# Inversion on 64-row diagonal blocks, 32-column matmul tiles, roots split between two engines, and a new order of the steps

## The chip, the core and the metric

The kernel runs on one core of one Trainium2 chip. A core has TensorE (PE in the profile; its weight loads are shown as PEld), VectorE (DVE), ScalarE (ACT), GpSimd (POOL) and SyncE (SP), which issues the DMAs. The metric is the device time of one launch in microseconds.

## What is computed

Two blocks run on x of 2048 tokens by 128 features, and each adds its layer-normalised result to x. The first is an online linear regression that is scanned over the tokens; the second is a stack of six layers, each with attention in windows of 32 tokens (16 heads of 64) and a gated feed-forward of 341 hidden units.

```python
def step(W, inp):
    xt, vt = inp
    y = xt @ W.T
    err = y - vt
    gW = scale * (err.T @ xt)
    return (W - eta * gW, y)
...
# attention, per layer
q = l2norm(q) * qs
k = l2norm(k) * ksc
q = q * cos * scale + rotate_half(q) * sin * scale
k = k * cos * inv + rotate_half(k) * sin * inv
out = local_attention(q, k, v)
...
# feed-forward, per layer
xn = (x - mu) / jnp.sqrt(var + 1e-05) * g + bln
a, gate = jnp.split(xn @ W1 + b1, 2, -1)
return a * jax.nn.gelu(gate, approximate=False) @ W2 + b2
...
for i in range(DEPTH):
    x = attn_layer(shift_tokens(x), ...) + x
    x = ffn_layer(shift_tokens(x), ...) + x
```

## The kernel before

The 2048 tokens are 16 tiles of 128 tokens; four tiles are a group.

**Prologue.** The scan is done in chunks of 128 tokens. Each chunk needs the inverse of a lower triangular 128x128 matrix, unit diagonal plus a scaled Gram matrix. `gram` makes the Gram matrices, VectorE turns them into starting matrices `c_mm`, and six rounds (`ROUNDS`) double the size of the inverted blocks from 2 to 128. In round r GpSimd multiplies the scaled Gram matrices by a level mask (`c_b`), TensorE multiplies them with the inverse so far (`below`, L355), ScalarE copies the product out of PSUM (`c_q`), TensorE multiplies from both sides (`update`, L371 and L372), and VectorE subtracts (L699). Four groups of four matrices go through each round. Then `apply_x` and `apply_v` use the inverses, and sixteen short `chain_w`, `chain_d` products carry W from chunk to chunk, the last twelve of them inside the first steps of the main loop.

**Main loop.** All five engines run a loop over s. For tile t of 96 (`STEPS`, six layers of 16 tiles) TensorE does in turn: `project` for k and for q (L245, x with a 128x1024 half of the weights, into `psq`), `turn` (L253, sixteen 64x64 transposes of q or of k), `mask` (L276, starts `pss` with the mask), `scores` (L284), `turn_p` (L253, transposes of the probabilities), `values` (L265, four banks, one per window of 32 tokens, which already hold v times the output weights), and `mix` (L300, probabilities times those). Once per group come `F` and `X` (four 128x128 transposes each, L521 and L530), `hidden` for three blocks of the gate (G0 to G2) and of the value (A0 to A2) of the feed-forward (L310), `narrow` (Z, L317) and, for the coming layer, one `merge` (H, L326), which multiplies a quarter of v's weights with the output weights.

The order within one s, and by how many steps each piece lags, is written out by hand for every engine. `take` hands out four PSUM banks (`ring`) in TensorE's order, so a use waits until the use four places earlier has been read out (`freed`). `psq` is one pair of banks for both projections: q of a tile waits until ScalarE has squared k (`sq_k`), and k of the next tile until it has squared q (`sq_q`).

VectorE multiplies both projections by the rotation tables (L782, L785, L841, L857), reduces squares, row maxima and sums. GpSimd adds the two rotary products (L1236, L1245), multiplies q and k by the inverse norms (L1290, L1294) and the probabilities by their inverse sums (L1240), makes the table `tab`, and computes the inverse norms `rn`: from a seed that ScalarE makes of the exponent bits, ten small instructions on 128x32 (L1269 to L1287). ScalarE copies PSUM banks to SBUF and does Square, Exp and Gelu. All data are f32 except the mask, which is bf16. One f32 matmul is two records in the trace (two passes), a transpose is one.

## Time and profile before

| | us |
|---|---|
| median of 3 runs | 1675.6 |
| lowest, highest | 1674.8, 1677.26 |
| profiled execution, whole time | 1674.12 |
| profiled execution, its span | 1672.3 |
| PE busy in the span | 1591.6 (95%) |
| POOL busy | 1386.3 (83%) |
| DVE busy | 1253.5 (75%) |
| ACT busy | 1080.7 (65%) |
| PE busy from 300 to 1500 us | 1194.84 of 1200 |

The span is what the trace covers, from the first to the last instruction; the whole time holds 1.8 us more. The share of busy time is an average over the prologue (up to the first `project` at 113.59 us), the main loop and a tail. A PE row of the timeline reads: start, length from the start of the first to the end of the last of its instructions, line, what is written and read, the part of the array used (rows*columns), the shape moved, and how many records. Its end lies some 0.16 us behind the moment at which the next instruction can enter, so costs are read from start to start.

### The profile page before, as it was taken

The numbers are of one execution on the slowest core, as the hardware profiler recorded it, in microseconds if no ns is written. First come the engines' busy times: TensorE is split into PE (matmuls) and PEld (weight loads), VectorE is DVE, ScalarE is ACT, GpSimd is POOL, SyncE is SP. The second block draws the span as 40 slices with busy tenths as digits, with TensorE's granted clock in tenths as the row PEclk, the third lists the DMA queues.
The fourth block names the chain that finished last, engine by engine and source line by source line (L and its number), as shares of the span: only waits on it lengthen the run. The fifth ranks groups of instructions, "written<-read, shape, count | busy, mean of one in ns | idle before, by whom it ended". The sixth has DMA issues, their size and how long they took to land.

```text
span 1672.3 us, 67208 instructions
## 1 busy us (share of the span) xinstructions
PE 1591.6 (95%) x29072; PEld 938.3 (56%) x29072; DVE 1253.5 (75%) x1683; ACT 1080.7 (65%) x1843; POOL 1386.3 (83%) x1726
## 2 busy tenths in 40 slices
PE   5986899999999999999999999999999999999994
PEld 4963455655555555565555555555555555555552
DVE  5447777777787787787787787777777787778863
ACT  3234766767766776766766767676766766766661
POOL 6318898988988988988998988988998998988971
PEclk9987999999999999999999999999999999999998
DMA  5000000010000010000010000010000000000000
GB/s 191 2 26 1 28 9 8 3 59 9 3 22 9 3 59 9 3 21 9 3 59 9 3 22 9 3 59 9 3 22 9 2 10 9 4 21 9 7 11 26
DMA packets 24534, 32.70 MB, mean 20 GB/s; under 512 B 2372, under 2 KB 21424, under 8 KB 23344
## 3 DMA queue, kind: packets, MB, share of 16 engines
q1 hardware_dynamic: 24240, 28.41, 5.2%
q8 instruction: 230, 3.77, 0.9%
q14 instruction: 64, 0.52, 0.1%
HBM read 21.06 MB, written 1.05 MB: 13 GB/s over the span
## 4 chain that ended last, share of the span: by engine, by line
PE 82%; POOL 8%; issue 5%; DVE 3%; ACT 1%; DMA 0%; SPq 0%; POOLq 0%; DVEq 0%; ACTq 0%
PE psq L245 19%; PE ring L265 18%; PE ring L253 9%; PE ring L300 9%; PE ring L310 8%; PE pss L284 7%; PE ring L317 3%; PE pss L276 1%; PE ring L326 1%; PE ring L355 1%; POOL qa L1290 1%; POOL qa L1245 1%; POOL qa L1236 1%; POOL qa L1294 1%; POOL pr L1240 1%
## 5 line engine op out<-in xcount | busy, mean ns | idle before, releaser
L245 PE MATMUL psq<-wqk,x0S 128*128 128x512 f32 x768 | 383.0, 622 | 5.5 <-ACT x0S L990 3.7
L265 PE MATMUL ring<-mh,x0S 128*32 128x512 f32 x3072 | 367.2, 595 | 0.4 <-ACT uT L1158 0.4
L1245 POOL TENSOR_TENSOR qa<-qa,qb 128x1024 f32<-128x1024 f32 x96 | 228.3, 2378 | 65.6 <-DVE qb L857 65.5
L1236 POOL TENSOR_TENSOR qa<-qa,qb 128x1024 f32<-128x1024 f32 x96 | 226.9, 2364 | 6.8 <-DVE qb L785 6.8
L245 PEld LDWEIGHTS psq<-wqk,x0S 128*128 128x128 f32 x768 | 136.1, 192 | 133.0 <-issue 117.2
L253 PEld LDWEIGHTS ring<-ident,qa 64*128 64x128 f32 x3072 | 110.5, 139 | 158.8 <-issue 104.7
L866 DVE TENSOR_REDUCE ss<-sq 128x16 f32<-128x1024 f32 x96 | 117.1, 1220 | 104.0 <-ACT sq L1062 104.0
L300 PE MATMUL ring<-u,pT 128*32 128x128 f32 x6144 | 187.6, 274 | 3.8 <-ACT pT L1129 3.5
L1290 POOL TENSOR_TENSOR qa<-qa,rn 128x1024 f32<-128x1024 f32 x96 | 182.7, 1903 | 7.5
L1240 POOL TENSOR_TENSOR pr<-pr,rden 128x1024 f32<-128x1024 f32 x96 | 184.0, 1916 | 2.0 <-DVE rden L814 2.0
L1294 POOL TENSOR_TENSOR qa<-qa,rn 128x1024 f32<-128x1024 f32 x96 | 183.2, 1908 | 0.0
L300 PEld LDWEIGHTS ring<-u,pT 128*32 128x32 f32 x6144 | 162.0, 110 | 27.2 <-issue 27.2
L284 PEld LDWEIGHTS pss<-kT,qT 64*32 64x32 f32 x12288 | 127.9, 105 | 83.3 <-issue 82.2
L782 DVE TENSOR_TENSOR qa<-psq,tab 128x1024 f32<-128x1024 f32 x96 | 117.2, 1221 | 75.4 <-PE psq L245 75.2
L1051 ACT COPY qT<-ring 128x512 f32<-128x512 f32 x96 | 56.3, 586 | 157.3 <-PE ring L253 157.3
L265 PEld LDWEIGHTS ring<-mh,x0S 128*32 128x32 f32 x3072 | 87.9, 109 | 123.1 <-issue 107.4
L841 DVE TENSOR_TENSOR qa<-psq,tab 128x1024 f32<-128x1024 f32 x96 | 117.2, 1221 | 51.1 <-PE psq L245 51.1
L310 PE MATMUL ring<-xh,w 128*128 128x512 f32 (+1 forms) x288 | 146.7, 620 | 1.4 <-ACT xh L1147 0.9
L284 PE MATMUL pss<-kT,qT 64*32 64x64 f32 x12288 | 144.5, 226 | 3.3 <-issue 3.3
L253 PE MATMUL ring<-ident,qa 64*128 64x64 f32 x3072 | 136.7, 229 | 6.4 <-POOL qa L1290 5.3
L1062 ACT ACTIVATE sq<-psq 128x1024 f32<-128x1024 f32 x96 | 98.3, 1023 | 67.7 <-DVE qb L857 67.7
L1167 ACT ACTIVATE sq<-psq 128x1024 f32<-128x1024 f32 x96 | 97.8, 1018 | 65.6 <-DVE qb L785 65.6
(161 smaller groups left out, 3005.1 us busy)
## 6 DMA issues: line engine op xcount, KB each, us to landing
wqk<-in_wqk SPq DMA_DIRECT2D x6, 1024.0 KB, 4.8
mvT<-in_mvT SPq DMA_DIRECT2D x6, 512.0 KB, 3.6
wo<-in_wo SPq DMA_DIRECT2D x6, 512.0 KB, 5.0
xf<-x SPq DMA_DIRECT2D x24, 128.0 KB
xf<-x SPq DMA_DIRECT2D x24, 127.0 KB
rope<-in_rope SPq DMA_DIRECT2D x1, 2048.0 KB, 10.2
w<-in_w SPq DMA_DIRECT2D x6, 341.0 KB, 7.1
xmid<-in_x SPq DMA_DIRECT2D x4, 256.0 KB, 5.4
```

The source lines that it names most:

```text
L245: return mm(psq[:, 512 * (n % 2):512 * (n % 2) + 512], x0S[:, tile * P:tile * P + P], wqk[:, l % 2, 512 * n:512 * n + 512], start=True, st ...
L253: last = tr(banks[r][:, 64 * blk:64 * blk + 64], src(blk)[rows], ident[rows, rows])
L265: last = mm(bank[WIN * g:WIN * g + WIN, :], x0S[:, tile * P + WIN * w:tile * P + WIN * w + WIN], mh[:, l % 2, g, :, :].rearrange("p j n -> ...
L284: last = mm(pss[WIN * w:WIN * w + WIN, 512 * r + KEYS * pair:512 * r + KEYS * pair + KEYS], qT[rows, pair, WIN * w:WIN * w + WIN], kT[rows ...
L300: last = mm(bank[WIN * w:WIN * w + WIN, 0:P], pT[:, half, b * P + WIN * w:b * P + WIN * w + WIN], u4[:, slot, v_w, b * P:b * P + P], start ...
L310: return mm(bank[0:n, :], w1[:, col:col + n], xnT[:, :], start=True, stop=True)
L782: v.tensor_tensor(a3[t % 2][:, 16:32, :], q3, tab[:, t % 2, 2, :].unsqueeze(1).broadcast_to([P, HEADS, HD]), ALU.mult)
L1236: g_.tensor_tensor(qa[:, t % 2, 1024:2048], qa[:, t % 2, 1024:2048], qb[:, 1024:2048], ALU.add).then_inc(sum_k, 1)
L1240: g_.tensor_tensor(p4[t % 2], p4[t % 2], rden[:, :].unsqueeze(1).unsqueeze(3).broadcast_to([P, 2, HEADS, WIN]), ALU.mult).then_inc(p_ready, 1)
L1245: g_.tensor_tensor(qa[:, t % 2, 0:1024], qa[:, t % 2, 0:1024], qb[:, 0:1024], ALU.add).then_inc(sum_q, 1)
L1290: g_.tensor_tensor(a3[t % 2][:, 16:32, :], a3[t % 2][:, 16:32, :], rn[:, 16:32].unsqueeze(2).broadcast_to([P, HEADS, HD]), ALU.mult).then_ ...
L1294: g_.tensor_tensor(a3[t % 2][:, 0:16, :], a3[t % 2][:, 0:16, :], rn[:, 0:16].unsqueeze(2).broadcast_to([P, HEADS, HD]), ALU.mult).then_inc ...
```

## The change

1. **Inversion on blocks of 64.** Rounds 0 to 4 work on the two 64x64 diagonal blocks of each matrix alone, at the two diagonal quarters of the array; the starting matrices, masks, copies and subtractions are 64 columns wide instead of 128. The last round makes only the off-diagonal block from the two inverted ones and writes it into `c_inv`, whose rest GpSimd has set to zero in round 1.
2. **Start.** TensorE's first transposes wait for the identity alone, VectorE's coefficient for eta and the level masks, and is asked for after the second group's statistics instead of the first's. The level masks are half as large.
3. **32-column tiles.** `project`, `hidden` and `narrow` issue each matmul as four (for the last 85 hidden units three) with 32 output rows each, as `values` and `mix` did before.
4. **Mask.** Eight 64-row, 32-column matmuls in the tiles that `scores` uses, issued directly before `scores`; before, two 32-row, 128-column ones were issued before `mix`, and two 128x128 ones in a layer's first tile.
5. **Merges** come in pairs that use the two 64-row halves of the array in turn, every second group.
6. **Roots.** Another polynomial: seven small instructions on ScalarE (the seed among them, which was there before) and three on GpSimd, instead of one and ten.
7. **New order.** Every engine's loop is written out anew and is five steps longer (`STEPS + 19` for `STEPS + 14`; the first projection is at s = 2). `project` for k stands near the end of a step, for q near the middle of the next. The three Gelus of a group stand at three places of ScalarE's loop instead of together. G0 to A2 are spread over the steps, Z moves to a step with X and F, and the final normalisation of the last layer's groups lies five steps behind its statistics.

```diff
             def project(t, n):
 
                 tile, l = t % TILES, t // TILES
-                return mm(psq[:, 512 * (n % 2):512 * (n % 2) + 512], x0S[:, tile * P:tile * P + P],
-                          wqk[:, l % 2, 512 * n:512 * n + 512], start=True, stop=True)
+                for w in range(NWIN):
+                    last = mm(psq[WIN * w:WIN * w + WIN, 512 * (n % 2):512 * (n % 2) + 512],
+                              x0S[:, tile * P + WIN * w:tile * P + WIN * w + WIN],
+                              wqk[:, l % 2, 512 * n:512 * n + 512], start=True, stop=True)
+                return last
 
...
             def mask(t):
 
-                for h in range(2):
-                    if t % TILES == 0:
-                        mm(pss[:, 512 * h:512 * h + 512], ident16[:, :], mask16[:, 1, :], start=True, stop=False)
-                    else:
-                        rows = slice(WIN * h, WIN * h + WIN)
-                        mm(pss[:, 512 * h:512 * h + 512], rep16[rows, :], mask16[rows, 0, :], start=True, stop=False)
+                for w in range(NWIN):
+                    for r in range(2):
+                        rows = slice(HD * r, HD * r + HD)
+                        mm(pss[WIN * w:WIN * w + WIN, 512 * r:512 * r + 512], rep16[rows, WIN * w:WIN * w + WIN],
+                           mask16[rows, int(t % TILES == 0 and w == 0), :], start=True, stop=False)
 
...
-                return mm(bank[0:n, :], w1[:, col:col + n], xnT[:, :], start=True, stop=True)
+                for c in range(0, n, WIN):
+                    m = min(WIN, n - c)
+                    last = mm(bank[c:c + m, :], w1[:, col + c:col + c + m], xnT[:, :], start=True, stop=True)
+                return last
 
...
                 for k in range(QUAD):
                     for j, (h0, n) in enumerate(HBLK):
                         n += j == 2
-                        last = mm(bank[:, k * P:k * P + P], uT[0:n, j, k * P:k * P + P], w2[0:n, j, :],
-                                  start=(j == 0), stop=(j == 2))
+                        for w in range(NWIN):
+                            rows = slice(WIN * w, WIN * w + WIN)
+                            last = mm(bank[rows, k * P:k * P + P], uT[0:n, j, k * P + WIN * w:k * P + WIN * w + WIN],
+                                      w2[0:n, j, :], start=(j == 0), stop=(j == 2))
                 return last
...
-            def merge(bank, j):
-
-                rows = slice(HD * (j % 2), HD * (j % 2) + HD)
+            def merge(what, l):
+
+                banks = [take("H%d" % j, l) for j in what]
+                for bank, n in banks:
+                    wait(pe, freed[bank], n)
                 for k in range(4):
-                    pair = 4 * (j // 2) + k
-                    last = mm(bank[:, k * P:k * P + P], mvT[rows, pair, :], wo[rows, pair, :], start=True, stop=True)
-                return last
+                    for j, (bank, n) in zip(what, banks):
+                        rows = slice(HD * (j % 2), HD * (j % 2) + HD)
+                        pair = 4 * (j // 2) + k
+                        last = mm(ring[bank][:, k * P:k * P + P], mvT[rows, pair, :], wo[rows, pair, :], start=True, stop=True)
+                        if k == 3:
+                            last.then_inc(filled[bank], 1)
...
-                    last = mm(quarter[g][:, k, :], c_xT[:, g, k, :], c_xT[:, g, k, :], start=True, stop=True)
+                    for o in range(2):
+                        for p in range(2):
+                            last = mm(blocks[g][BOTH[p], o, k, :], c_xT[:, g, k, BOTH[p]], c_xT[:, g, k, BOTH[p ^ o]],
+                                      start=True, stop=True)
...
-                    last = mm(rbank[g][:, k, :], c_b[r % 2][:, g, k, :], c_mm[:, g, 1, k, :], start=True, stop=True)
+                    if r < ROUNDS - 1:
+                        for rows in BOTH:
+                            last = mm(rblock[g][rows, k, :], c_b[r % 2][rows, g, k, :], c_mm[rows, g, 1, k, :], start=True, stop=True)
+                    else:
+                        last = mm(rblock[g][LO, k, :], c_g[HI, g, 1, k, :], c_inv[HI, g, k, HI], start=True, stop=True)
                 last.then_inc(a_Q, 1)
...
                     if r < ROUNDS - 1:
-                        mm(bank[:, k * P:k * P + P], c_q[:, g, k, :], c_mm[:, g, 0, k, :], start=True, stop=True)
-                    last = mm(bank[:, 512 + k * P:512 + k * P + P], c_mm[:, g, 0, k, :], c_q[:, g, k, :],
-                              start=True, stop=True)
+                        for rows in BOTH:
+                            mm(blocks[g][rows, 0, k, :], c_q[rows, g, k, :], c_mm[rows, g, 0, k, :], start=True, stop=True)
+                        for rows in BOTH:
+                            last = mm(blocks[g][rows, 1, k, :], c_mm[rows, g, 0, k, :], c_q[rows, g, k, :], start=True, stop=True)
+                    else:
+                        last = mm(blocks[g][LO, 1, k, :], c_mm[LO, g, 0, k, :], c_q[LO, g, k, :], start=True, stop=True)
                 last.then_inc(a_U, 1)
...
-                    lo = 512 * (r == ROUNDS - 1)
-                    both = c_mm[:, g].rearrange("p t k n -> p (t k n)")[:, lo:]
-                    v.tensor_tensor(both, both, pair[g % 2][:, lo:], ALU.subtract).then_inc(a_m, 1)
+                    if r < ROUNDS - 2:
+                        v.tensor_tensor(c_mm[:, g], c_mm[:, g], blocks[g], ALU.subtract).then_inc(a_m, 1)
+                    elif r == ROUNDS - 2:
+                        wait(dve, s_iz, 1)
+                        v.tensor_tensor(c_mm[:, g, 0], c_mm[:, g, 0], blocks[g][:, 0], ALU.subtract)
+                        for rows in BOTH:
+                            last = v.tensor_tensor(c_inv[rows, g, :, rows], c_mm[rows, g, 1], blocks[g][rows, 1], ALU.subtract)
+                        last.then_inc(a_m, 1)
+                    else:
+                        v.tensor_scalar(c_inv[LO, g, :, HI], blocks[g][LO, 1], -1.0, None, ALU.mult).then_inc(a_m, 1)
...
-                if g == 0:
-                    dve.wait_ge(s_const, 16 * NCONST)
+                if g == 1:
+                    dve.wait_ge(s_level, 32)
...
+                    nc.scalar.activation(rg[:, :].bitcast(I32), ssc[:, :].bitcast(I32), ACT.Copy, bias=SEED,
+                                         scale=-0.5).then_inc(seed_ready, 1)
+                    act.wait_ge(seed_ready, t + 1)
+                    wait(act, rb_ready, t)
+                    nc.scalar.activation(ra[:, :], rg[:, :], ACT.Square).then_inc(rg_ready, 1)
...
+                    act.wait_ge(rb_ready, t + 1)
+                    nc.scalar.activation(rs1[:, :], rb[:, :], ACT.Square, bias=rcon[:, 0:1]).then_inc(rs_ready, 1)
+                    nc.scalar.activation(rs2[:, :], rb[:, :], ACT.Square, bias=rcon[:, 1:2]).then_inc(rs_ready, 1)
+                    wait(act, rp_ready, t)
+                    act.wait_ge(rs_ready, 2 * t + 1)
+                    nc.scalar.activation(rf1[:, :], rs1[:, :], ACT.Copy, bias=RB)
+                    act.wait_ge(rs_ready, 2 * t + 2)
+                    nc.scalar.activation(rf2[:, :], rs2[:, :], ACT.Copy, bias=R4 * RD, scale=R4).then_inc(rf_ready, 1)
...
+                    pool.wait_ge(rg_ready, t + 1)
+                    wait(pool, rs_ready, 2 * t)
+                    g_.tensor_tensor(rb[:, :], ra[:, :], ssc[:, :], ALU.mult).then_inc(rb_ready, 1)
...
+                    pool.wait_ge(rf_ready, t + 1)
+                    g_.tensor_tensor(rp[:, :], rf1[:, :], rf2[:, :], ALU.mult).then_inc(rp_ready, 1)
+                    pool.wait_ge(rp_ready, t + 1)
+                    g_.tensor_tensor(rn[:, :], rg[:, :], rp[:, :], ALU.mult).then_inc(rn_ready, 1)
...
-                    g_.tensor_tensor(ra[:, :], rn[:, :], rn[:, :], ALU.mult).then_inc(r_step, 1)
...
-                    g_.tensor_tensor(rn[:, :], rc[:, :], ra[:, :], ALU.mult).then_inc(r_step, 1)
```

TensorE, one step of the main loop. The first name is the tensor written, then what it reads; 32x512 is output rows by columns. Before, starting at the mask of one tile:

```order
L276 MATMUL pss<-mask,rep 128x512 x2
L300 MATMUL ring<-u,pT 32x128 x32
L265 MATMUL ring<-mh,x0S 32x512 x4
L253 MATMUL ring<-ident,qa 128x64 x16
L245 MATMUL psq<-wqk,x0S 128x512 x2
L253 MATMUL ring<-ident,qa 128x64 x16
L265 MATMUL ring<-mh,x0S 32x512 x12
L284 MATMUL pss<-kT,qT 32x64 x64
L253 MATMUL ring<-ident,pr 128x64 x16
```

and now, starting at a hidden block (L323 is `hidden`, L311 `mix`, L265 the transposes, L255 `project`, L277 `values`, L286 the mask, L295 `scores`):

```order
L323 MATMUL ring<-xh,w 32x512 x4
L311 MATMUL ring<-u,pT 32x128 x32
L265 MATMUL ring<-ident,qa 128x64 x16
L255 MATMUL psq<-wqk,x0S 32x512 x8
L265 MATMUL ring<-ident,qa 128x64 x16
L277 MATMUL ring<-mh,x0S 32x512 x4
L323 MATMUL ring<-xh,w 32x512 x4
L277 MATMUL ring<-mh,x0S 32x512 x4
L286 MATMUL pss<-mask,rep 32x512 x8
L295 MATMUL pss<-kT,qT 32x64 x64
L265 MATMUL ring<-ident,pr 128x64 x16
L255 MATMUL psq<-wqk,x0S 32x512 x8
```

The 128-wide projections and hidden blocks have gone, and the mask has moved from in front of `mix` to in front of `scores`.

ScalarE, a step with Gelus. Before, all three stand behind one table load (`pr` is Exp, `uT` Gelu, `sq` the square that frees `psq`):

```order
L1110 COPY pT<-ring 128x8x64
L1129 COPY pT<-ring 128x8x64
L1134 ACTIVATE pr<-pr 128x1024
L1158 ACT_TABLE_LOAD
L1158 ACTIVATE uT<-ring,par 128x512 x2
L1158 ACTIVATE uT<-ring,par 85x512
L1167 ACTIVATE sq<-psq 128x1024
L1174 ACTIVATE kT<-kT,kfac 128x8x32
```

and now, the end of one such step and the start of the next:

```order
L1223 COPY u<-ring 128x512
L1228 ACTIVATE sq<-psq 128x1024
L1085 ACT_TABLE_LOAD
L1085 ACTIVATE uT<-ring,par 85x512
L1093 COPY kT<-ring 128x8x64
L1099 COPY kT<-ring 128x8x64
```

The third Gelu has a table load of its own between the square and the copies of k; the whole program has 92 table loads where it had 46.

## Rows read from the trace of the kernel before

**Rows 1.** The page: span, and the chain that ended last, by engine.

```profile
span 1672.3 us, 67208 instructions
PE 82%; POOL 8%; issue 5%; DVE 3%; ACT 1%; DMA 0%; SPq 0%; POOLq 0%; DVEq 0%; ACTq 0%
```

**Rows 2.** Busy time by stretch: us, PE, PEld, DVE, ACT, POOL, PEclk, DMA, GB/s.

```profile
44.00:90.00 46.00, 46.00 (x414) 46.00 (x413) 21.50 (x19) 11.04 (x20) 14.89 (x12) 1.00 0.01 1
300.00:1500.00 1200.00, 1194.84 (x22912) 679.35 (x22914) 940.76 (x1161) 837.50 (x1414) 1068.00 (x1314) 1.00 0.05 16
```

**Rows 3.** Timeline of TensorE over one step: start, length, line, tensors, array part.

```profile
1012.86 1.04 PE L265 MATMUL ring<-mh,x0S 128*32 128x512 f32 x8
1013.84 0.71 PE L253 MATMUL ring<-ident,qa 64*128 64x64 f32 x16
1014.48 1.98 PE L245 MATMUL psq<-wqk,x0S 128*128 128x512 f32 x4
1016.30 1.02 PE L310 MATMUL ring<-xh,w 128*128 128x512 f32 x2
1017.25 0.71 PE L253 MATMUL ring<-ident,qa 64*128 64x64 f32 x16
1017.89 2.78 PE L265 MATMUL ring<-mh,x0S 128*32 128x512 f32 x24
1020.60 1.49 PE L284 MATMUL pss<-kT,qT 64*32 64x64 f32 x128
1022.02 1.12 PE L310 MATMUL ring<-xh,w 128*128 128x512 f32 x2
1023.08 0.71 PE L253 MATMUL ring<-ident,pr 64*128 64x64 f32 x16
1023.72 1.98 PE L245 MATMUL psq<-wqk,x0S 128*128 128x512 f32 x4
1025.63 0.39 PE L276 MATMUL pss<-mask,rep 32*128 32x512 bf16 x2
1025.95 1.96 PE L300 MATMUL ring<-u,pT 128*32 128x128 f32 x64
1027.72 1.04 PE L265 MATMUL ring<-mh,x0S 128*32 128x512 f32 x8
```

**Rows 4.** Timeline of TensorE: the product Z of a group.

```profile
1040.55 2.84 PE L317 MATMUL ring<-w,uT 128*128 128x128 f32 x24
```

**Rows 5.** Groups of instructions by line: all merges (busy us, mean ns).

```profile
L326 PE MATMUL ring<-wo,mvT 64*128 64x128 f32 x192 | 27.9, 285 | 0.6 <-issue 0.6
```

**Rows 6.** Timeline of ScalarE: copy of the probabilities, table load, Exp, square.

```profile
1024.30 0.59 ACT L1129 COPY pT<-ring 128x512 f32<-128x512 f32 x1
1024.91 1.28 ACT L1134 ACT_TABLE_LOAD   x1
1026.21 1.06 ACT L1134 ACTIVATE pr<-pr 128x1024 f32<-128x1024 f32 x1
...
1028.13 1.02 ACT L1167 ACTIVATE sq<-psq 128x1024 f32<-128x1024 f32 x1 [0.86 <-DVE qb L785]
```

**Rows 7.** Timeline of GpSimd: first of ten small root instructions, and what follows them.

```profile
1022.61 0.24 POOL L1269 TENSOR_TENSOR ra<-rn 128x32 f32<-128x32 f32 x1
...
1025.82 1.90 POOL L1290 TENSOR_TENSOR qa<-qa,rn 128x1024 f32<-128x1024 f32 x1
```

**Rows 8.** Timeline of VectorE: the second rotary product of k.

```profile
1026.88 1.22 DVE L785 TENSOR_TENSOR qb<-psq,tab 128x1024 f32<-128x1024 f32 x1
```

**Rows 9.** The chain that ended last, in the prologue: start us, us, what.

```profile
5.51 6.38 DMA mh<-in_bv
...
45.85 3.57 PE ring L355 x32
...
88.73 3.57 PE ring L355 x32
...
113.59 2.08 PE psq L245 x2
```

More of the change, by code:

```diff
@@ L387, in apply_x @@
                 for k in range(QUAD):
[L388 removed]
+                    last = mm(rbank[bank][:, k, :], c_xn[:, g, k, :], c_inv[:, g, k, :], start=True, stop=True)
                 last.then_inc(filled[bank], 1)
@@ L427, in features @@
                 last.then_inc(filled[bank], 1)
-            def first_merge(j):
-                bank, n = take("H%d" % j, 0)
-                pe.wait_ge(mw_ready, 32)
-                wait(pe, freed[bank], n)
-                merge(ring[bank], j).then_inc(filled[bank], 1)
+            pe.wait_ge(s_ident, 16)
             turn_in(0)
@@ L625, in _ @@
-                if i >= 0:
-                    bank, n = take("A1", i)
-                    wait(pe, freed[bank], n)
-                    hidden(ring[bank], 1, 0).then_inc(filled[bank], 1)
-                t = s - 2
-                if 0 <= t < STEPS:
-                    banks = [take("P0", t), take("P1", t)]
-                    pe.wait_ge(p_ready, t + 1)
-                    for bank, n in banks:
-                        wait(pe, freed[bank], n)
-                    turn_p([ring[bank] for bank, n in banks], t)
@@ L1186, in _ @@
+                    rows = HBLK[0][1]
+                    nc.scalar.activation(uT[0:rows, 0, :], ring[bank][0:rows, :], ACT.Gelu,
+                                         bias=par[0:rows, i // GROUPS, 5:6]).then_inc(freed[bank], 1)
         @block.gpsimd
```

948 lines of the change are left out of this document (489 added, 459 removed).

## The prediction

> **What bounds the kernel now.** I read the shares of the chain first: TensorE carries 82% of it, "issue" 5%, GpSimd 8% [rows 1]. Then the busy time by stretch: from 300 to 1500 us TensorE is busy 1194.84 of 1200 us, while GpSimd has 1068, VectorE 941 and ScalarE 838 [rows 2]. So in the loop nothing but TensorE's own stream sets the pace, and a change is worth what it takes out of that stream, as long as no new wait appears. Third, the timeline of one step, read from start to start [rows 3]. From the values at 1012.86 to the next at 1027.72 are 14.86 us; two hidden blocks in it took 0.95 (1016.30 to 1017.25) and 1.06 (1022.02 to 1023.08), which leaves 12.85 for a step without extras. Last, the chain in the prologue, which takes 113.59 us before the first projection [rows 9].
>
> **32-column tiles for projections and hidden blocks.** The row of four full-width passes is 1.98 long, that of two 1.12: one more pass costs 0.43. The row of 24 tile records (six rounds of four) is 2.78, that of eight (two rounds) 1.04: one more round costs 0.435 [rows 3]. So the arithmetic is no faster in tiles. By the Trainium skill, "TensorEngine Tiling (Array Packing)", section Theoretical Speedup, packing gains where a dimension is 64 or less; by that rule this edit, whose dimensions are 128, brings nothing, and for the passes the trace agrees. What is left to gain are the changes between array shapes. Beyond its passes, the projection in front of the mask takes 1.91 - 1.72 = 0.19, that in front of a turn or hidden block 0.10; values in front of a turn 0.98 - 0.86 = 0.12, in front of the scores 2.71 - 2.58 = 0.13; a hidden block that comes after scores and before a turn 1.06 - 0.86 = 0.20, one that comes after a projection 0.09 [rows 3]. So leaving a shape costs about 0.12, and entering the full array about 0.1 more. A turn (0.64) and the scores (1.41) can't be divided that way; I give them the same 0.13. A step has nine changes of shape before (mask to mix, values to turn, turn to q, q to turn, turn to values, values to scores, scores to turn, turn to k, k to mask) and seven after, since mix, values, projections and hidden blocks now share one shape and mask and scores another. Lower bound: two changes at 0.13, 0.26. Upper bound: also 0.1 for each of the two projections that no longer enter the full array, 0.46. I take 0.35, because rows 3 show the entry cost for hidden blocks but for projections only mixed with the neighbour's. The mask's own time (0.32 to the mix, of which 0.21 is half of an f32 pass) stays; eight tiles side by side stream it once. Four steps of a group: **1.4 us**.
>
> **Other edits of the group.** A merge costs 27.9 / 24 = 1.16 [rows 5]; two of them on the two row halves run like the turn's pairs, so a pair costs about one: between 0.3 and 0.58 saved per group, I take 0.4. Z's 24 records take 2.84 [rows 4], about 0.112 each; as tiles they run like the mix, 64 records or 16 rounds in 1.77, 0.111 each [rows 3]: 24 rounds 2.66, 0.1 saved. Against that, X now stands between mix and turn and F between turn and projection, each a visit to the full array at about 0.2, where they stood behind a full-width projection at no cost; the hidden block behind the scores, at 0.2, is gone: minus 0.2. Sum 1.4 + 0.4 + 0.1 - 0.2 = **1.7 us per group**. All of it lies on the path. The stream sets the end for about 23 of the 24 groups (filling and emptying the pipeline are set by latencies, and I take the new depth of lags there as neutral, plus or minus 6): 39 us.
>
> **Roots.** Ten small GpSimd instructions take 1025.82 - 1022.61 = 3.21 us per step [rows 7], three will take 1.0. GpSimd is off the path, so its 2.2 us bring nothing themselves; the cover is TensorE's stream. Six more small ones on ScalarE, some 0.25 each, raise its 838 of 1200 us (10.8 per step) to 12.3. The chain from turned probabilities to the next turn of k is copy 0.59, seed, square, GpSimd's product, four on ScalarE, two on GpSimd, scaling 1.90: about 5.2 us with their hand-overs (0.08 between two rows of GpSimd). TensorE has between the two the k projection, U3, U0, a hidden block and the mix, 1.86 + 0.86 + 0.86 + 0.86 + 1.77 = 6.2. It fits by 1.0.
>
> **New order, and what is queued on ScalarE.** Gelus at three places double the table loads, from 46 to 92, two more per group. A load takes 1.30 from its start to that of the Exp behind it [rows 6]. Take E as the end of TensorE's U3. ScalarE copies U3 from E+0.2 to E+0.8, loads the table to E+2.1, does Exp (1.06) to E+3.15, copies U0 to E+3.6 and squares k (1.02; neighbours overlap by 0.1) to E+4.55. `psq` then is free for q. TensorE wants it after U0, a hidden block, the mix and the turn: 0.86 + 0.86 + 1.77 + 0.64 + 0.12 = E+4.25. It waits 0.3, in the two steps of a group whose Exp comes behind a Gelu. In one of these a third load and Gelu stand between the square and the copies, to about E+6.55; the bank they free is wanted by the turn of q at E+6.4: 0.15 more. Sum 0.7 per group, 16 us. In the other two steps the square is ready 1.0 early. Bounds: 0 (the table could load during another wait) and 1.4 (the same shortfalls doubled, since each of them is a small difference of long sums). VectorE's rotary products stay at 1.22 each [rows 8]; two of them and the square of q (1.02) fit between the projection of q and that of k with 2 us to spare.
>
> **Prologue.** (a) The first transposes wait for the last constant, which lands at 5.51 + 6.38 = 11.9 [rows 9]; now for the identity and for the first group's normalised rows: 0 to 6 us, I take 5. (b) The weight rows L355 from 45.85 to 88.73 are four rounds, 10.72 us each [rows 9], in which TensorE is busy 46 of 46 us at a granted clock of 1.00, its 2.4 GHz level [rows 2]: 96 records of 128 columns, 0.112 each. After, 192 records of 64 columns, in pairs on two diagonal quarters. The nearest row is the turn, eight pairs of 64 columns in 0.64 less 0.13, 0.064 a pair [rows 3]: 96 pairs are 6.1, at best (half of a 128-column record) 5.4. Saved 4.6 to 5.3, I take 4.9: 20 for four rounds. VectorE and GpSimd, 21.5 and 14.9 of 46 us there, halve too and stay covered. (c) Round 0 and the start of round 1, from 11.9 to 45.85, are short TensorE pieces between VectorE's and GpSimd's products; these become half as wide: 34 us less the 5 of (a) that just shifts; between 8 and 18 less, I take 13. (d) The last round: 3.57 for `below` and as much for `update`, each about halved or better, 4. Together **42 us**, on the path entirely, bounds 28 and 50.
>
> **Sum.** Against the profiled execution: span 1672.3, 1.8 us around it. 42 + 39 - 16 = 65 us less: span 1607, time 1609; the profiled execution lies 1.5 under the median of 1675.6, so the median becomes **1610 us**.
>
> **Rivals.** (1) No new wait on ScalarE: the loads fall into its idle time. For it: ScalarE is idle 30% of the loop [rows 2]. Against: the load stands in order between U3's copy and the Exp. 1610 - 16 = 1594. (2) The diagonal quarters don't run side by side, or the thinner work leaves the engine at its 1.2 GHz level: a round stays near 11. For it: no row of before has 64x64 parts. Against: transposes on two row halves and values on four column parts do run side by side. 1610 + 20 = 1630. (3) The shape changes are not what costs, and the step keeps its 12.85: 1.4 x 23 = 32 more, 1642. Against: 0.09 and 0.20 for the same hidden block in two places [rows 3]. (4) Slower: the root chain, now with six hand-overs between ScalarE and GpSimd and as many within them, becomes the loop's clock. It fits by 1.0 only; it decides once it is 1.0 + 65/96 = 1.7 us longer than laid out, that is if a hand-over costs 0.25 instead of 0.08 over some ten of them. At 0.27 each it would be 1.9 longer, 0.9 per step, 86 less the 65: about 1697. Against: ScalarE rows follow GpSimd's and VectorE's within 0.1. (5) Slower too: a change of table costs more than the load's row. If the engine also stood still around it for as long again, q would wait 1.6 twice a group and the turn 1.5: 4.8 a group, 110 - 81 = 29 above before, 1705. The row speaks against it: 1.28 long, 0.02 behind the copy, 0.02 ahead of the Exp [rows 6]. The Trainium skill, "ScalarE: Activation LUTs", section What ACT_TABLE_LOAD costs, gives about 2.66 us for a switch, a drain included; by that rule this rival holds, and this trace shows 1.30.
>
> **How the numbers follow.** Forecast (1598 to 1624) 0.46; rival 1 0.26; rival 2 0.12; rival 3 0.08; rival 4 0.04; rival 5 0.02; another slower one or no change 0.02. The range goes from rival 1 with the prologue at its better bound (1594 - 8, rounded to 1585) to rival 3, 1643. About 0.2% of the time, 3.4 us, is what a measurement of this kernel can tell from no change. Faster 0.93, same 0.01, slower 0.06.
>
> **What would show each step.** The first projection at 70 to 73 us instead of 113.6; weight loads of `below` some 5.8 apart per round; a step without extras near 12.5, and four steps about 1.0 shorter; a projection of two banks 1.72 to 1.75 between neighbours of its own shape; TensorE idle, or a lengthened first pass of q, behind ScalarE's square only in steps with a table load; 92 table loads; GpSimd's busy time down by about 160 us and ScalarE's up by about 200. The prediction is wrong if rounds stay at 10 us, if idle time of TensorE in the loop exceeds 1.5 us per group, or if the steps take 12.85 as before.

## The result and the profile after

| | before | after |
|---|---|---|
| median | 1676.4 us (4 runs) | 1627.4 us (4 runs) |
| lowest, highest | 1674.8, 1678.9 | 1622.7, 1628.3 |
| ratio after/before, 95% interval | | 0.9701 [0.9678, 0.9723] |
| span of the profiled execution | 1672.3 us | 1620.9 us |

49 us faster; 65 were forecast. The first page lines of the changed kernel, answering [rows 1] (span, busy time by engine, chain by engine):

```profile
span 1620.9 us, 79276 instructions
PE 1532.9 (95%) x35024; PEld 853.4 (53%) x35024; DVE 1243.1 (77%) x1693; ACT 1219.7 (75%) x2368; POOL 1220.0 (75%) x1051
PE 75%; issue 9%; ACT 7%; DVE 1%; POOL 1%; DMA 0%; SPq 0%; ACTq 0%; DVEq 0%; POOLq 0%
```

TensorE's share of the chain fell from 82% to 75%, and ScalarE, which had 1%, now has 7%. The same in the busy times by stretch, answering [rows 2] (us, PE, PEld, DVE, ACT, POOL, PEclk, DMA, GB/s): inversion rounds, then the loop.

```profile
34.00:54.00 20.00, 20.00 (x692) 20.00 (x689) 9.92 (x17) 6.36 (x16) 4.81 (x7) 1.00 0.02 5
300.00:1500.00 1200.00, 1174.11 (x27354) 641.65 (x27346) 946.63 (x1174) 956.87 (x1844) 951.82 (x780) 1.00 0.05 16
```

TensorE now stands idle 25.9 of 1200 us in the loop; before it was 5.2. That is 1.07 more per group of tiles.

**Where the 49 us come from.** The start of the k projection of a tile, before minus after: tile 0 35.3 us (113.59 to 78.28), tile 4 38.5, tile 8 44.2, tile 16 47.1, tile 48 45.6, tile 92 49.0, end 51.4. So the prologue brought 35, the filling of the pipeline 12, and the long loop almost nothing: its mean period per group (tiles 16 to 92, 19 groups) is 61.84 us before and 61.75 after. (These are the profiled executions; that of the changed kernel is the fastest of its four, so the differences end at 51.4 and not at 49.)

One step of TensorE after the change, answering [rows 3]:

```profile
898.86 1.92 PE L255 MATMUL psq<-wqk,x0S 128*32 128x512 f32 x16
900.60 1.90 PE L277 MATMUL ring<-mh,x0S 128*32 128x512 f32 x16
902.32 0.60 PE L323 MATMUL ring<-xh,w 128*32 128x512 f32 x3
...
903.18 1.92 PE L311 MATMUL ring<-u,pT 128*32 128x128 f32 x62
905.28 0.71 PE L265 MATMUL ring<-ident,qa 64*128 64x64 f32 x16 [0.18 <-ACT u L1223]
906.12 1.92 PE L255 MATMUL psq<-wqk,x0S 128*32 128x512 f32 x16
908.16 0.71 PE L265 MATMUL ring<-ident,qa 64*128 64x64 f32 x16
908.81 1.07 PE L277 MATMUL ring<-mh,x0S 128*32 128x512 f32 x8
```

The projection next to values takes 1.74 from start to start. The `mix` (1.75 where nothing delays what follows) takes 2.10 here, because the turn of k waits; the turn takes 0.84 instead of 0.64, because q waits; and q takes 2.04 instead of 1.85 in front of the next turn. ScalarE at that place, answering [rows 6]:

```profile
901.71 0.59 ACT L1213 COPY u<-ring 128x512 f32<-128x512 f32 x1 [0.60 <-PE ring L277]
902.32 1.28 ACT L1217 ACT_TABLE_LOAD   x1
903.61 1.06 ACT L1217 ACTIVATE pr<-pr 128x1024 f32<-128x1024 f32 x1
904.57 0.57 ACT L1223 COPY u<-ring 128x512 f32<-128x512 f32 x1
905.04 1.03 ACT L1228 ACTIVATE sq<-psq 128x1024 f32<-128x1024 f32 x1
906.09 1.28 ACT L1085 ACT_TABLE_LOAD   x1
```

The copy of U0 ends at 905.14 and the turn starts at 905.28; the square ends at 906.07 and q starts at 906.12. TensorE's waits in the loop (300 to 1500 us; total, times, longest) name both, and a third thing, "issue", time for which the profile shows nothing that was waited for:

```profile
PEld psq L255 <- ACT sq L1228: 10.2, 39, 0.3
PE ring L265 <- issue: 7.2, 6, 1.6
PE ring L265 <- ACT u L1223: 6.9, 37, 0.3
```

Last, the prologue, answering [rows 9], and two of GpSimd's three root instructions with the scaling of k behind them, answering [rows 7]:

```profile
12.48 1.97 PE L356 MATMUL ring<-ident,wqk 128*128 128x128 f32 x8 [12.48 <-DMA mh<-in_bv]
...
32.39 2.08 PE L382 MATMUL ring<-qa,u 64*64 64x64 f32 x64
...
78.28 2.96 PE L255 MATMUL psq<-wqk,x0S 128*32 128x512 f32 x16 [0.41 <-ACT x0S L1033]
```

```profile
901.19 0.25 POOL L1332 TENSOR_TENSOR rp<-rf 128x32 f32<-128x32 f32 x1 [0.22 <-ACT rf L1195]
901.52 0.25 POOL L1334 TENSOR_TENSOR rn<-rg,rp 128x32 f32<-128x32 f32 x1
901.85 1.91 POOL L1352 TENSOR_TENSOR qa<-qa,rn 128x1024 f32<-128x1024 f32 x1
```

### The profile page after: what moved, and what is told of

Same layout as the page of the kernel before. It is cut to its first block, busy times and chain, and to the rows that moved or that the text cites. A ratio compares the mean times of both kernels' runs of the same rounds, so it can differ in the third digit from the quotient of the medians.

```text
span 1620.9 us, 79276 instructions
## 1 busy us (share of the span) xinstructions
PE 1532.9 (95%) x35024; PEld 853.4 (53%) x35024; DVE 1243.1 (77%) x1693; ACT 1219.7 (75%) x2368; POOL 1220.0 (75%) x1051
## 3 DMA queue, kind: packets, MB, share of 16 engines
HBM read 20.80 MB, written 1.05 MB: 13 GB/s over the span
## 4 chain that ended last, share of the span: by engine, by line
PE 75%; issue 9%; ACT 7%; DVE 1%; POOL 1%; DMA 0%; SPq 0%; ACTq 0%; DVEq 0%; POOLq 0%
PE psq L255 21%; PE ring L277 18%; PE ring L265 9%; PE pss L295 7%; PE ring L311 5%; PE ring L323 5%; PE ring L333 4%; ACT sq L1228 3%; PE pss L286 2%; ACT u L1223 1%; ACT pr L1217 1%; PE ring L651 1%; ACT L1217 1%; PE ring L566 1%; PE ring L346 1%
## 5 line engine op out<-in xcount | busy, mean ns | idle before, releaser
L277 PE MATMUL ring<-mh,x0S 128*32 128x512 f32 x3072 | 401.4, 597 | 1.9 <-DVE uT L826 1.5
L255 PE MATMUL psq<-wqk,x0S 128*32 128x512 f32 x3072 | 381.6, 606 | 9.5 <-ACT sq L1129 1.7
L311 PE MATMUL ring<-u,pT 128*32 128x128 f32 x6144 | 198.4, 273 | 0.2 <-ACT u L1213 0.2
L311 PEld LDWEIGHTS ring<-u,pT 128*32 128x32 f32 x6144 | 176.3, 110 | 40.9 <-issue 39.4
L277 PEld LDWEIGHTS ring<-mh,x0S 128*32 128x32 f32 x3072 | 94.9, 109 | 177.5 <-issue 159.9
L265 PEld LDWEIGHTS ring<-ident,qa 64*128 64x128 f32 x3072 | 112.8, 139 | 111.2 <-issue 107.5
L899 DVE TENSOR_REDUCE den<-pr 128x16 f32<-128x1024 f32 x96 | 116.8, 1216 | 65.5 <-ACT pr L1217 64.6
L255 PEld LDWEIGHTS psq<-wqk,x0S 128*32 128x32 f32 x3072 | 82.1, 110 | 152.1 <-issue 127.6
L323 PE MATMUL ring<-xh,w 128*32 128x512 f32 (+1 forms) x1056 | 156.3, 603 | 0.9 <-ACT xh L1204 0.9
L1158 ACT COPY pT<-ring 128x512 f32<-128x512 f32 x96 | 56.3, 587 | 125.6 <-PE ring L265 125.5
L265 PE MATMUL ring<-ident,qa 64*128 64x64 f32 x3072 | 137.2, 229 | 11.6 <-ACT u L1223 7.8
L295 PEld LDWEIGHTS pss<-kT,qT 64*32 64x32 f32 x12288 | 138.8, 105 | 6.8 <-issue 1.7
L295 PE MATMUL pss<-kT,qT 64*32 64x64 f32 x12288 | 140.7, 225 | 1.2 <-issue 1.1
L1322 POOL TENSOR_TENSOR rb<-ra,ssc 128x32 f32<-128x32 f32 x96 | 24.4, 254 | 156.0 <-ACT ra L1168 155.9
```

The lines of the kernel that those rows point to most:

```text
L255: last = mm(psq[WIN * w:WIN * w + WIN, 512 * (n % 2):512 * (n % 2) + 512], x0S[:, tile * P + WIN * w:tile * P + WIN * w + WIN], wqk[:, l % ...
L265: last = tr(banks[r][:, 64 * blk:64 * blk + 64], src(blk)[rows], ident[rows, rows])
L277: last = mm(bank[WIN * g:WIN * g + WIN, :], x0S[:, tile * P + WIN * w:tile * P + WIN * w + WIN], mh[:, l % 2, g, :, :].rearrange("p j n -> ...
L295: last = mm(pss[WIN * w:WIN * w + WIN, 512 * r + KEYS * pair:512 * r + KEYS * pair + KEYS], qT[rows, pair, WIN * w:WIN * w + WIN], kT[rows ...
L311: last = mm(bank[WIN * w:WIN * w + WIN, 0:P], pT[:, half, b * P + WIN * w:b * P + WIN * w + WIN], u4[:, slot, v_w, b * P:b * P + P], start ...
L323: last = mm(bank[c:c + m, :], w1[:, col + c:col + c + m], xnT[:, :], start=True, stop=True)
```

## Experiments

"The changed kernel" is the one after the change. Every ratio is to the kernel before, with its 95% interval. The last column but one is the mean period of a group in the loop, in the profiled execution (tiles 16 to 92); the last is the start of the first projection.

| kernel | median us | ratio | group us | first projection |
|---|---|---|---|---|
| before | 1676.4 | | 61.84 | 113.59 |
| changed | 1627.4 | 0.9701 [0.9678, 0.9723] | 61.75 | 78.28 |
| b_pro | 1631.5 | 0.9743 [0.9728, 0.9757] | 61.57 | 77.23 |
| b_tiles | 1669.4 | 0.997 [0.9958, 0.9982] | 61.84 | 112.86 |
| a_wide | 1689.4 | 1.008 [1.0062, 1.0097] | 64.44 | 77.08 |
| a_oldroots | 1637.5 | 0.9777 [0.9761, 0.9793] | 61.94 | 76.75 |
| b_roots | 1705.7 | 1.0187 [1.017, 1.0204] | 63.26 | 113.03 |
| a_nogelu | 1599.9 | 0.9548 [0.9528, 0.9568] | 60.84 | 78.97 |
| b_nogelu | 1675.0 | 1.0001 [0.9989, 1.0013] | 61.93 | 114.46 |
| a_early | 1600.9 | 0.9554 [0.9537, 0.9571] | 60.77 | 76.78 |
| a_sqk | 1712.4 | 1.0212 [1.0192, 1.0232] | 65.49 | 77.35 |
| a_es | 1602.9 | 0.9566 [0.9543, 0.9588] | 60.81 | 78.13 |
| a_shift16 | 1608.1 | 0.9588 [0.9571, 0.9605] | 60.87 | 76.88 |
| a_shift32 | 1606.2 | 0.9581 [0.9566, 0.9597] | 60.74 | 77.88 |

### The prologue alone (b_pro)

The edit is parts 1 and 2 of the change in the kernel before, whose loop stays. Its core:

```diff
-                    last = mm(rbank[g][:, k, :], c_b[r % 2][:, g, k, :], c_mm[:, g, 1, k, :], start=True, stop=True)
+                    if r < ROUNDS - 1:
+                        for rows in BOTH:
+                            last = mm(rblock[g][rows, k, :], c_b[r % 2][rows, g, k, :], c_mm[rows, g, 1, k, :], start=True, stop=True)
```

> The kernel before with parts 1 and 2 of the change alone: the inversion on 64-row blocks and the start; its loop stays as it was. Read from the two traces, the first projection comes 35.3 us earlier in the changed kernel, and the loop behind it does not depend on how it was reached. Theory A (the prologue's gain arrives whole): first projection near 78, time 1676 - 35 = 1641. Theory B (the first steps after it wait for something with a clock of its own, a load or the chain of W, so that part of it is given back): above 1650.

Measured 1631.5. The prologue's gain arrives whole: 36.4 us at the first projection, 37.8 at tile 16. The span is 43.3 shorter; the rest appears in the loop, where TensorE is idle 1.85 of 1200 us instead of 5.2, with fewer stalls of the kind "issue" (below: they sum to 0.7 us in that stretch, before to 4.7). The edit changes nothing in the loop, so this part is hardly the prologue's arithmetic; that it comes from where the stalls fall was not tested on this kernel. **With the prologue alone the kernel has nearly all of the gain: everything else in the change together is worth 4 us (0.9743 to 0.9701).**

### The tiles, in the old order and in the new (b_tiles, a_wide)

```diff
-                return mm(psq[:, 512 * (n % 2):512 * (n % 2) + 512], x0S[:, tile * P:tile * P + P],
+                for w in range(NWIN):
+                    last = mm(psq[WIN * w:WIN * w + WIN, 512 * (n % 2):512 * (n % 2) + 512],
```

b_tiles does this, and the same in `hidden` and `narrow`, to the kernel before; a_wide undoes it in the changed kernel.

> The kernel before with the projections, hidden blocks and Z in 32-column tiles, nothing else. In its order they do not stand beside mix or values, so no change of shape goes away; what can go is the extra cost of entering the full array. By the prediction's term (0.1 for each of two projections and two hidden blocks in three that enter it): 0.25 per step, 24 us, 1652. By the changed kernel's own rows (a projection between turns 1.85 instead of 1.91, Z 2.64 instead of 2.77): 0.12 to 0.15 per step, 12 to 14 us, 1662 to 1664. Rival (the form brings nothing by itself, only the neighbourhood counts): 1676.

> The changed kernel with projections, hidden blocks and Z at full width again. By the prediction's terms a step loses two changes of shape and two entries, 0.35 to 0.46, but in two steps of a group TensorE waits for ScalarE anyway and a part is hidden: 0.25 to 0.35 per step, 1650 to 1660. If the tiles bring less, as the loop's unchanged period lets one think (0.1 per step): 1636. Rival (they bring nothing): 1627.

Measured: b_tiles has the period of before to 0.01 us and gains 5 us (3 to 7 by its interval), of which its profiled execution shows 1.8, all of it by tile 16. The equal periods hide a small gain. In b_tiles TensorE is idle 8.35 of 1200 us instead of 5.2, and the granted clock is at its lower level from 621.8 to 625.2. The median of each of a group's four steps leaves such stops out; these medians add up to 61.45 us in b_tiles and 61.68 before. a_wide is 62 us slower than the changed kernel and slower than before, nearly twice what the highest expectation said. TensorE's rows of a_wide:

```profile
957.96 1.92 PE L274 MATMUL ring<-mh,x0S 128*32 128x512 f32 x16
959.82 1.13 PE L318 MATMUL ring<-xh,w 128*128 128x512 f32 x2
960.87 1.95 PE L308 MATMUL ring<-u,pT 128*32 128x128 f32 x64
962.76 0.71 PE L262 MATMUL ring<-ident,qa 64*128 64x64 f32 x16
```

Values 1.86, hidden block 1.05, mix 1.89 from start to start. The chain of the changed kernel through the same three (start us, us, what):

```profile
886.49 1.72 PE ring L277 x16
888.21 0.86 PE ring L323 x8
889.07 1.75 PE ring L311 x64
```

So one hidden block at full width between two neighbours in tiles costs 0.47, spread over all three. The new order has such places six times a group, and between the projection of k and the values in every step. **The tile form by itself brings little (0.2 us per group, 5 us in all); what it saves depends on what stands beside it, and the new order is faster than the old only with it.** By the same medians the changed kernel takes 61.26, of which 1.1 is waiting for ScalarE (60.17 in a_nogelu, below), and a_wide 62.77, whose matmuls show no wait for ScalarE (its weight loads still do, 0.2 before q). So the rows of full width cost 1.5 per group more, and up to 2.6 where those waits are set aside; six times 0.47 is 2.8. A part of a_wide's 2.7 us per group, 0.5, is longer "issue" idle (21.3 against 11.3 us from 300 to 1500).

### The roots (a_oldroots, b_roots)

```diff
-                    g_.tensor_tensor(rb[:, :], ra[:, :], ssc[:, :], ALU.mult).then_inc(rb_ready, 1)
...
-                    g_.tensor_tensor(rp[:, :], rf1[:, :], rf2[:, :], ALU.mult).then_inc(rp_ready, 1)
...
+                    g_.tensor_tensor(ra[:, :], rn[:, :], rn[:, :], ALU.mult).then_inc(r_step, 1)
...
+                    g_.tensor_tensor(rn[:, :], rc[:, :], ra[:, :], ALU.mult).then_inc(r_step, 1)
```

This is a_oldroots, the changed kernel with the old roots; b_roots is the opposite in the kernel before. Its four instructions behind GpSimd's product stand on ScalarE behind the copy of P1, ahead of the Exp.

> The changed kernel with the roots as they were before (ten small instructions on GpSimd, one on ScalarE). Theory A: it loses what the roots bring in the first steps, 8 to 12 us, and nothing in the loop, since the copy of U3 behind the moved instructions waits for TensorE in any case (0.60 us idle): 1635 to 1640. Rival 1 (the roots bring nothing): 1627. Rival 2 (the longer chain on GpSimd makes the turn of k wait in every step, by 0.3 or more): the loop gains 0.3 per step, 1660 and above.

> The kernel before with part 6 alone: seven small root instructions on ScalarE and three on GpSimd instead of one and ten. Theory A: in the kernel before, GpSimd is what the chain runs through in steps 3 to 14 (its rows stand in the chain from 170 us on), so 2.2 us less of it per step shorten these steps by about 1 us each, 8 to 12 us in all, and the loop behind them, where TensorE is busy 1194.8 of 1200 us, does not move: 1664 to 1668. The prediction's reading (GpSimd's relief has no term anywhere): 1676. Rival: ScalarE, which now waits for GpSimd's product ahead of its Exp, hands the delay to TensorE, and the time rises above 1680.

a_oldroots: 10 us slower than the changed kernel, 8.2 of it by tile 16, 0.19 per group in the loop. This is theory A, and it explains some two thirds of what the filling gained. The place is narrow: from the k projection of tile 3 to that of tile 9 the kernel before takes 94.3 us, a_oldroots 90.8, the changed kernel 83.3, and the other kernels with its roots and tiles (a_nogelu, a_early, a_es and the shifts) 83.2 to 85.9. The first three tiles are less clear: a_oldroots takes 2.2 us more for them, but at a granted clock of 0.66 from 76 to 130 us, where the changed kernel has 0.77. The kernel before shows why, in its chain through these steps:

```profile
189.25 0.65 POOL ra L1269
...
194.74 1.90 POOL qa L1294
...
196.88 1.04 POOL lrstd L1197
...
198.51 2.33 POOL qa L1236
200.84 0.60 POOL pr L1240
...
202.68 2.36 POOL qa L1245
205.04 0.69 POOL tab L1250
```

From 170 to 255 us each step follows from GpSimd's own work, with layer-norm roots (`lrstd`) added to it: there GpSimd sets the pace, not TensorE.

b_roots refutes the same theory for the old order: 31 us slower, and even from tile 3 to tile 9 only 1.3 us faster than before (93.0). So in the filling too the roots pay only together with the new order, which without them brings 3.5 us there. TensorE's longest waits in its loop are for the copy of P1 (total, times, longest):

```profile
PE ring L303 <- ACT pT L1137: 15.0, 18, 1.9
```

From 1227 to 1250 us its chain touches TensorE nowhere; it runs through ScalarE's and GpSimd's root instructions and GpSimd's other work. A ScalarE instruction that waits for GpSimd holds up the Exp behind it, and GpSimd's product stands behind its other work. The prediction's rival 4 (the root chain as what sets the loop's pace) is thus real, in the old order with this placement; in the new one it isn't.

### The table loads (a_nogelu, b_nogelu, a_early)

The two `nogelu` kernels:

```diff
-                    nc.scalar.activation(uT[0:rows, 2, :], ring[bank][0:rows, :], ACT.Gelu,
+                    nc.scalar.activation(uT[0:rows, 2, :], ring[bank][0:rows, :], ACT.Identity,
```

and a_early:

```diff
+                if 0 <= s - 4 < STEPS and (group_at(s, 11) >= 0 or group_at(s, 12) >= 0):
+                    nc.scalar.activation(junk[:, 0:1], rcon[:, 0:1], ACT.Exp)
                 t = s - 5
                 if 0 <= t < STEPS:
                     bank, n = place["P0", t]
```

> The changed kernel with Identity in place of Gelu: the Gelu of the feed-forward is left out, the instructions stay, and with them go all table loads but the first. Theory A (the loads' time on ScalarE delays U0's bank by 0.35 and the square of k by 0.2 in the two steps of a group with an Exp behind a Gelu): 1.1 us per group, 25 us, 1602. The prediction's term (0.7 per group): 1611. Rival (TensorE's idle time in the loop has another cause): above 1622.

> The kernel before with Identity in place of Gelu, which is left out; one load of a table is left instead of 46. Theory A: TensorE is busy 1194.8 of 1200 us in its loop, so the loads cost nothing there: 1674 to 1676. Rival (the loads cost 1.3 each in either kernel): 46 times 1.3, 1616.

> The changed kernel with an Exp of one column ahead of the copy of P0 in the steps that have a Gelu since the last Exp. It draws the table load forward into the 1.6 us in which ScalarE waits for TensorE there. Nothing is left out. Theory A: the 1.1 us per group that the loads cost go away, 25 us less than the changed kernel: 1602. Rival (the load only changes its place and the copies of P0 and the roots behind it come late): no gain, 1627 or more.

Without loads the changed kernel takes 1599.9, 27.5 less, and the kernel before takes what it took. With the loads kept and 45 of them drawn forward it takes 1600.9. ScalarE in a_early:

```profile
900.06 0.59 ACT L1141 COPY u<-ring 128x512 f32<-128x512 f32 x1
900.67 1.28 ACT L1153 ACT_TABLE_LOAD   x1
901.96 0.20 ACT L1153 ACTIVATE junk<-rcon 128x1 f32<-128x1 f32 x1
902.29 0.59 ACT L1161 COPY pT<-ring 128x512 f32<-128x512 f32 x1
...
905.03 0.59 ACT L1216 COPY u<-ring 128x512 f32<-128x512 f32 x1 [0.60 <-PE ring L278]
905.51 1.06 ACT L1220 ACTIVATE pr<-pr 128x1024 f32<-128x1024 f32 x1
```

The load lies where ScalarE waited for TensorE anyway, the Exp follows the copy of U3 at once, and TensorE's waits name ScalarE no more. **Theory A holds, in its mechanism and its size, and the kernel with this one instruction more beats both, 0.9554 against 0.9701.**

### The square ahead of the Exp (a_sqk)

```diff
-                    act.wait_ge(p_shifted, t + 1)
-                    nc.scalar.activation(pr[:, t % 2, :], pr[:, t % 2, :], ACT.Exp, scale=QK_SCALE).then_inc(exp_done, 1)
                     bank, n = place["U0", t]
...
                     nc.scalar.activation(sq[:, 1, :], psq[:, :], ACT.Square).then_inc(sq_k, 1)
+                t = s - 4
+                if 0 <= t < STEPS:
+                    act.wait_ge(p_shifted, t + 1)
+                    nc.scalar.activation(pr[:, t % 2, :], pr[:, t % 2, :], ACT.Exp, scale=QK_SCALE).then_inc(exp_done, 1)
```

> The changed kernel with one move on ScalarE: U0's copy and the square of k stand ahead of the Exp instead of behind it. All 92 table loads stay where an Exp follows a Gelu. Theory A (the loads cost only because the bank of U0 and the square are queued behind them): the same gain as without loads, 22 to 27 us less than the changed kernel, 1600 to 1605. Rival 1 (the later Exp makes the probabilities late for their turn, which has 2 to 3 us to spare, or the copies of k late): half of it or less, above 1613. Rival 2 (the cost of a load is something else than its time in ScalarE's queue): 1627.

A miss by over 100 us: 1712.4, 85 slower than the changed kernel. TensorE's waits in its loop:

```profile
PE ring L265 <- DVE x L923: 34.4, 19, 2.2
PE ring L265 <- ACT uT L1085: 24.0, 19, 1.6
```

and VectorE in a step of it:

```profile
972.42 1.22 DVE L899 TENSOR_REDUCE den<-pr 128x16 f32<-128x1024 f32 x1 [3.46 <-ACT pr L1230]
973.56 0.74 DVE L909 SCALAR_TENSOR_TENSOR uT<-ring,par,uT 128x512 f32<-128x512 f32 x1
974.22 0.24 DVE L915 RECIPROCAL rden<-den 128x16 f32<-128x16 f32 x1
974.38 0.23 DVE L923 TENSOR_TENSOR x<-ring,x0T 128x128 f32<-128x128 f32 x1
```

I had priced the late Exp at its own consumers, the probabilities, which do have room. But VectorE takes its instructions in order: behind the sum that waits 3.46 us for the Exp stands the addition `x`, which reads out the bank of `mix`, and the turn of q needs that bank. The second wait is the same on ScalarE itself: the third Gelu (`uT`, L1085) and its load now stand behind the late Exp, and the turn of q wants the bank that this Gelu reads. U0's bank and the square are early in this kernel (no wait of TensorE names them), and it doesn't help.

### The first wait, and where instruction blocks begin (a_es, a_shift16, a_shift32)

```diff
             mm, tr = nc.tensor.matmul, nc.tensor.transpose
-            wait(pe, s_const, 16 * NCONST)
...
             pe.wait_ge(s_ident, 16)
+            for _ in range(32):
+                mm(ring[0][0:32, 0:32], ident[0:32, 0:32], ident[0:32, 0:32], start=True, stop=True)
```

a_es is a_early without the first wait; the two `shift` kernels add the loop to it, with 16 and with 32.

> The early Exp of one column, and besides TensorE's first wait, for the last three constants, taken away (the products that need them have waits of their own). Theory A: the first transposes start when the first normalised rows are ready, at 9.8 to 11.4 instead of 12.5, so everything is 1 to 2.5 us earlier: 1598 to 1600. Rival (ScalarE's and GpSimd's first products set the pace anyway): no change, 1601.

> The kernel of a_es with 16 small matmuls more on TensorE, 64 instructions, ahead of its first transposes, where it is idle. They add nothing to the path; what they move is where in the loop the blocks of 256 instructions begin that the instruction queue brings. Theory A (TensorE's stalls behind the scores, 1.0 to 1.8 us each and some 12 us in all, are waits for such a block, hence depend on where its border falls): total stall time and the time change by several us, either way. Rival (the stalls belong to a place in the program or to other transfers): within 2 us of a_es and stalls in the same steps.

> As a_shift16 with 32 small matmuls, 128 instructions, half a block. Theory A: the stalls fall into other steps than in a_es and in a_shift16, and their sum differs from both. Rival: within 2 us of a_es, stalls in the same steps.

a_es: no gain (the rival). Its transposes start at 10.20, released by ScalarE's normalised rows and no longer by a constant (10.66 in a_early), but the Gram products behind them start at 12.80, where a_early has them at 12.63.

The shifts: the stalls do move. A stall here is a place where two of TensorE's records start more than 0.75 us apart. From 300 to 1500 us, and without the rows at a lowered clock, a_es has 15 of them, each of the shifts 11. The first four lie in a_es at 414.71, 475.53, 536.71, 569.24, in a_shift16 at 389.70, 452.22, 558.74, 619.13, in a_shift32 at 327.09, 375.85, 435.67, 784.44. Their sum doesn't change: from 300 to 1500 us "issue" on TensorE adds up to 13.1, 13.4 and 13.5 us. The medians differ by 5 and 3 us; the intervals of a_es and of the shifts overlap, so I don't call that a difference. Theory A holds in that the stalls move with the instruction count; its second half, that their sum would change, doesn't.

## Why the prediction was right, and where not

**The bound.** TensorE's stream is the bound of the loop, as said. It was not from tile 3 to tile 9, where the chain of the kernel before runs through GpSimd (170 to 255 us). "Filling neutral, plus or minus 6" is the first step that failed: 12 us came from there, 11 of them between these tiles, and some 8 are lost again with the old roots, which I had given no term because I looked for their cover in the loop alone.

**Prologue, 42 forecast, 35.3 measured.** (a) Start: 5 forecast, nothing measured. The change has the wait for the identity, but an older line, `wait(pe, s_const, ...)` at the head of TensorE's program, stands ahead of it and still waits for all constants; the first transposes start at 12.48 behind `mh<-in_bv` (11.93 before). I had read the diff and not the lines around it. a_es shows that even without that line nothing comes of it. (b) Rounds: the first `below` of each stands 5.60 to 5.65 apart (32.39, 38.04, 43.64, 49.24, that of the last round at 54.68) against 10.72; over four of them 20.6 are saved; forecast 20. The clock is granted in full and the diagonal quarters do work side by side, so rival 2 is out. (c) From the first transposes to round 1: 33.9 before [rows 9], 19.9 after, 14.0; forecast 13. (d) From the start of the last round to the first projection: 24.9 before, 23.6 after, 1.3; forecast 4.

**Tiles and other edits, 1.7 per group forecast.** Read without load waits, the loop takes 60.84 instead of 61.84 (a_nogelu): 1.0. With the 0.4 per group that "issue" grew (4.7 us before and 12.2 in a_nogelu, in 19.4 groups) the rows themselves give 1.4: a plain step's pieces in the chain add up to 12.57, before 12.85. Mechanism right (rival 3 out by a_wide), size a fifth too high. The step of [rows 3] that I had not thought through: the gain is one of order and form together, 0.2 by form alone.

**ScalarE, 0.7 per group forecast, 16 us.** Measured 26.5 (a_early) and 27.5 us (a_nogelu), 0.9 to 1.0 per group. The layout of ScalarE's queue was right to 0.1: with E at 901.5, U0's copy ends at E+3.6 and the square at E+4.55, as laid out. What was mis-sized is TensorE's side: I compared the square with q and never U0's copy with the turn of k, which wants its bank at E+3.4. That is 0.35 more, twice a group. The waits stand only in steps with a load, and the third one (q's turn behind the Gelu G2) measures 0.19 against 0.15 forecast. The Trainium skill, "ScalarE: Activation LUTs", section What ACT_TABLE_LOAD costs, gives about 2.66 us for a switch, of which some 1.28 is the load and the rest a drain. The 91 loads in the loop here last 1.28 each with 0.02 around them, so the load agrees and no drain shows. With 27.5 us for all loads together, rival 5 is out.

**Sum.** 42 + 39 - 16 = 65 were forecast; measured are 35 (prologue), 12 (filling), 2 to 4 (loop and end). The forecast of 1610 stood on a loop that brings 23 us net and brings 2: 0.7 per group too much from the stream and from "issue" together, and 0.3 too little taken off for ScalarE. Rival 1 (no wait) is nearly what a_early reaches, 1600.9 for 1594. GpSimd lost 166 us of busy time (160 forecast), ScalarE gained 139 (200 forecast).

## What to carry to other kernels

An in-order queue's price is paid by whatever stands behind the instruction that waits: go through the queue item by item and ask of each when its reader wants it, not only of the one you moved. A table load, or any fixed cost on an engine that has idle time elsewhere, can be drawn into that idle time by a one-column instruction. And read which engine the chain follows in each stretch: relief for an engine that is covered in the loop can pay where the pipeline fills, if the order lets it through (the same roots gained nothing in the old order).

## What the runs showed of the hardware

**TensorE seems to wait for its own instructions.** The records of DMA transfers in the changed kernel have 276 packets of 16 KB of the kind "instruction". 276 times 256 is 70,656, and TensorE has 70,048 instructions, so one packet holds 256 and nearly all are TensorE's. From 300 to 1500 us there are 11 places where two of TensorE's records start more than 0.75 us apart with nothing waited for (in 8 of them it is idle for more than 0.75), and each stop begins 0.9 to 1.8 us after such a packet starts (it takes 0.9 to 1.4). They lie in the scores or at most 1.9 us behind, where TensorE goes through 272 instructions in some 1.6 us; packets that arrive elsewhere in a step leave hardly a mark. The kernel before has 3 such stops. Where the stops end says more: in the two kernels, a_es and the shifts together there are 51, and each ends 1.24 to 1.58 us after the latest packet has been transferred, whether it is 0.8 or 2.6 us long, while a packet comes only about every 5.6 us. The two longest, in a_shift32, begin before their packet does, as if TensorE had run out of instructions. That the packets cause the stops was not shown by taking one away; that the stops move with the instruction count was (the shifts). The Trainium skill, "Runtime: NRT & Kernel Launch", section Instruction fetch mechanics, has blocks of 16 KiB or 256 instructions whose cost is mostly hidden: the size agrees, and some 11 us in 1200 are not hidden here.

**A stop can cost the clock as well.** In a_shift16 TensorE is busy 0.92 of 2.5 us around its stall at 389.70, and the granted clock falls to its 1.2 GHz level for a part of the next 4.5 us (us, PE, PEld, DVE, ACT, POOL, PEclk, DMA, GB/s):

```profile
389.00:391.50 2.50, 0.92 (x44) 0.71 (x29) 2.38 (x4) 1.63 (x6) 1.53 (x3) 1.00 0.00 0
391.50:396.00 4.50, 4.48 (x28) 1.49 (x32) 1.68 (x2) 1.37 (x5) 4.11 (x5) 0.62 0.01 4
```

There four rounds of 512 columns in four 32-column tiles follow each other at 0.82 to 0.85 us instead of 0.43. In a_shift32 the same comes behind both of its longest stops: the granted clock is at the lower level from 329.6 to 333.0 and from 1063.4 to 1066.8 us. It doesn't come behind every long stop: the one at 1409.07 in a_shift16, 2.1 us from start to start, is followed by a full clock.
